# Expert results in a routed feed-forward layer: indirect scatter to (token, choice) rows in place of indirect gathers

## Chip, cores and metric

One core of a Trainium2 chip runs the whole kernel. The metric is the device time of one execution in microseconds (us).

## What is computed

A decoder layer on 2048 tokens (32 sequences of 64) of width 256: self-attention, cross-attention to a compressed context, then a mixture of 8 experts, each added to the residual x. The change touches the last part:

```python
probs = softmax(layernorm(x) @ Wr)                # 8 experts
topk_w, topk_idx = top_k(probs, 2)
topk_w = topk_w / sum(topk_w)
for i in range(8):
    h = silu(xn @ Wg[i]) * (xn @ Wu[i])           # 256 -> 256
    output += w_i * (h @ Wd[i])                   # w_i is 0 where i was not chosen
x = x + output
```

## The kernel before

The five engines' programs are written out by hand (functions tensor, vector, scalar, gpsimd, sync) and meet at semaphores; each runs its own in order. 16 token tiles of 128 tokens pass through attention in blocks of four. Routing of block b (`route_step`) runs beside the cross-attention of the next block: `route_slots` gives each (token, choice) a row in the DRAM table `slots`, where each expert has a region, and POOL scatters the normalised tokens there (`scatter`, two indirect DMAs a token tile, 32 in all). Part 0 is blocks 0 to 2 (12 token tiles), part 1 is block 3. `table(q)` works out on VectorE which expert and which row of `slots` each of the part's expert tiles has (31 tiles in part 0, 15 in part 1), on one partition. `slots` is filled beforehand with arbitrary numbers, so that a tile's unused rows hold something finite.

The expert stage is a loop over 46 expert tiles i of 128 rows. Work on tile i is spread over several iterations:

- PE: `gate_up(i)` (6 matmuls of 512 columns), transposes of h of tile i-1 (`h_T`), `down(i-2)` (6 of 256 columns), transposes of the rows of tile i+2 (`x_T`).
- ACT: `silu(i)`, `h_high(i-1)`, `copy_out(i-2)` into `ys[i % 4]`, `x_high(i+2)`.
- DVE: `gated(i)`, `h_low(i-1)`, `x_low(i+2)`, routing steps of block 3, then from iteration COMBINE_AT = 37 on `combine(i-37)`: two scalar_tensor_tensor instructions add the two weighted result rows of a token tile to x.
- SP: `store(i-2)` of `ys` back to the same rows of `slots`, then `load(i+6)` of the rows of tile i+6 into `xs[(i+6) % 4]` as soon as `x_T(i+2)` has read that buffer (`w.wait_ge(t_xT, i - 3)` inside `load`). Every eighth tile (8, 16, 24, 31, 39) SP first reads a run of row numbers into registers (`load_run`, L342); PE does so for the weights' offsets. `result` stores the finished x.
- POOL: the eight scatters of block 3, one a tile, then `gather(t)`: two indirect DMAs a token tile fetch the rows of its two choices from `slots` into eight buffers `gb`. For t below 12 it waits for the stores of part 0 and is paced by `x_T(36 + t)`; for t of 12 to 15 it waits for the stores of all 46 tiles.

All helpers record one line each: matmuls stand under L354, transposes under L363. L1439 is gated, L1443 h_low, L1433 x_low, L1451 combine, L1713 silu, L1718 h_high, L1723 copy_out, L1708 x_high, L1932 store, L1927 load, L1938 result, L1810 scatter, L1846 gather, L1885 the fill of `slots`.

Of the kernel before, what the change touches and what calls it, by code (L numbers as in the profile page):

```python
# [36 lines left out]
def constants():  # L37
# [36 lines left out]
    c["iota"] = np.tile(np.arange(TILES[0])[None, :], (P, 1))  # L74
    c["power"] = np.tile(np.array([[-0.5] * NT + [0.5] * NT]), (P, 1))
# [70 lines left out]
def decoder(nc, a, const_dram, const_at, out):  # L146
    with ExitStack() as ctx:
# [69 lines left out]
        after_folds = max(w2.at, keep.at + 4 * E * WE + 18 * 4 * D)  # L217
# [8 lines left out]
        past, pastgap = compared("past", [1, TILES[0], E]), compared("pastgap", [1, TILES[0], E])  # L226
# [12 lines left out]
        mxhat = s4("mxhat", [P, 4, D])  # L239
        mxT = s4("mxT", [P, KD, 512])  # L240
        full = s4("full", [1, E, CAP[0] // P])
        ntile = s4("ntile", [1, E])
        upto = s4("upto", [1, E, E])
        ends = s4("ends", [1, E])
        gap = s4("gap", [1, E])
        expert = s4("expert", [1, TILES[0]])
        rowf = s4("rowf", [1, TILES[0]])
        eoff = s4("eoff", [1, sum(TILES)], I32)
        row = s4("row", [1, sum(TILES)], I32)
# [28 lines left out]
        xs = [s6(f"xs{i}", [P, D]) for i in range(4)]  # L278
# [9 lines left out]
        gb = [s7(f"gb{i}", [P, D]) for i in range(8)]  # L288
        assert s7.at <= after_scores
        slots = [nc.dram_tensor(f"slots{i}", (ROWS[i], D), F32, kind="Internal").ap() for i in range(2)]  # L290
# [6 lines left out]
        d_xs, d_ys, d_gb = ([sem(f"d_{n}{i}") for i in range(k)] for n, k in (("xs", 4), ("ys", 4), ("gb", 8)))  # L297
# [33 lines left out]
        t_xT, t_xh, t_xl, t_proj, t_silu, t_gu, t_hT, t_hh, t_hl, t_down, t_y, t_comb = (  # L331
            sem("t_xT"), sem("t_xhigh"), sem("t_xlow"), sem("t_proj"), sem("t_silu"), sem("t_gu"), sem("t_hT"), sem("t_hhigh"),
            sem("t_hlow"), sem("t_down"), sem("t_y"), sem("t_comb"))
# [12 lines left out]
        RK = 24  # L346
# [569 lines left out]
        def vector(e):  # L916
# [271 lines left out]
            def route_norm(b):  # L1188
                w.wait_ge(r_rstd, b + 1)
                w.wait_ge(d_scat, 128 * b)  # L1190
                w.wait_ge(r_xT, b)
                for t in range(4):
                    last = e.tensor_scalar(mxhat[:, t, :], tile(4 * b + t), mmv[:, t, 0:1], mrstd[:, t:t + 1], ALU.subtract, ALU.mult)
                last.then_inc(r_xhat, 1)
# [55 lines left out]
            def route_slots(b):  # L1250
                at = RK * b
                pos = pos_bank(b)[:, 32:64].rearrange("p (t n) -> p t n", n=E)
                base = C("ebase")[:, E * (b == 3):E * (b == 3) + E]
                w.wait_ge(r_pos, b + 1)
                e.tensor_tensor(slot[:, :, :], pos, in_tiles(base, 4), ALU.add).then_inc(r_route, 1)
                w.wait_ge(r_route, at + 18)
                for k in range(2):
                    e.scalar_tensor_tensor(pick[k][:, :, :], rank[:, :, :], float(k), slot[:, :, :], ALU.is_equal, ALU.mult).then_inc(r_route, 1)
                for k in range(2):
                    w.wait_ge(r_route, at + 19 + k)  # L1260
                    e.tensor_reduce(slotf[:, :, k], pick[k][:, :, :], AX, ALU.add).then_inc(r_route, 1)
                w.wait_ge(r_route, at + 22)
                e.tensor_copy(index[:, 4 * b:4 * b + 4, :], slotf[:, :, :]).then_inc(r_route, 1)

            def route_count(b):
                w.wait_ge(r_route, RK * b + 23)
                count = pos_bank(b)[0:1, 64:64 + E].rearrange("p (n o) -> p n o", o=1).broadcast_to([1, E, CAP[0] // P])
                e.tensor_tensor(full[:, :, :], count, in_tiles(C("fill")[0:1], E), ALU.is_gt).then_inc(r_route, 1)
# [6 lines left out]
            def table_ends(q):  # L1275
# [5 lines left out]
                e.tensor_tensor(upto[:, :, :], C("le")[0:1].rearrange("p (i j) -> p i j", j=E), in_tiles(ntile[:, :], E), ALU.mult)  # L1281
# [4 lines left out]
                number = C("iota")[0:1, 0:n].rearrange("p (n o) -> p n o", o=1).broadcast_to([1, n, E])  # L1286
                e.tensor_tensor(past[:, 0:n, :], number, in_tiles(ends[:, :], n), ALU.is_ge).then_inc(r_tab, 1)

            def table_rows(q):
                n, at = TILES[q], 10 * q  # L1290
                mine = slice(FIRST[q], FIRST[q] + n)
                w.wait_ge(r_tab, at + 4)
                e.tensor_reduce(expert[:, 0:n], past[:, 0:n, :], AX, ALU.add)
# [5 lines left out]
                e.scalar_tensor_tensor(row[:, mine], C("iota")[0:1, 0:n], float(P), rowf[:, 0:n], ALU.mult, ALU.add).then_inc(r_tab, 4)  # L1299
# [135 lines left out]

            def gated(i):
# [22 lines left out]
            for i in range(tiles + 2):  # L1459
# [282 lines left out]
        def gpsimd(e):  # L1742
# [62 lines left out]
            def scatter(b, n):  # L1805
                q = int(b == 3)
                t, k = divmod(n, 2)
                w.wait_ge(r_route, RK * b + 23)
# [53 lines left out]
        def sync(e):
# [130 lines left out]
```

## Time and profile before

| | |
|---|---|
| median of 3 runs | 711.88 us (711.37 to 712.47) |
| the profiled execution | 710.46 us |
| its span, first to last instruction | 708.7 us |
| mean granted TensorE clock | 0.962 |
| busy: PE / DVE / ACT / POOL | 638.3 / 494.5 / 348.8 / 242.1 us |
| DMA | 61.54 MB, mean 87 GB/s |

A busy time is a sum over stages with different limits; times of the trace count from the span's start. The expert loop's first tile starts near 554 us, its last result tile is copied out at 690 us.

### The profile page before, as it was taken

What the parts mean: (1) busy time and instruction counts of PE and PEld (TensorE: products, weight loads), DVE (VectorE), ACT (ScalarE), POOL (GpSimd) and SP (SyncE); (2) the same over time, 40 slices, a digit from 0 to 9 for tenths busy, and PEclk for the clock granted to TensorE, in tenths of its full rate; (3) what the DMA queues carried; (4) which work ended last, traced back from release to release, by engine and by line L of the source; (5) the groups of instructions that cost most, each with busy time, mean ns of one, the idle gap of its engine ahead of it and who ended that gap; (6) DMA issues with size and microseconds to landing.
All of it is one profiled execution on the core that took longest, in us unless ns stands there. A gap on an engine that the chain in (4) does not pass through costs nothing.

```text
span 708.7 us, 15301 instructions
## 1 busy us (share of the span) xinstructions
PE 638.3 (90%) x5650; PEld 474.7 (67%) x5650; DVE 494.5 (70%) x1152; ACT 348.8 (49%) x1207; POOL 242.1 (34%) x219
## 2 busy tenths in 40 slices
PE   3787999998899999999999999999979999999850
PEld 2466777777787757667577666775656788888740
DVE  4998989995566878449884698736978737443652
ACT  1477989997660017501374014722288464554420
POOL 2112000000008528534287453773454001302644
PEclk9999999996999999999999999999989999999985
DMA  8699920000000000000001200011171223533544
GB/s 294 161 355 420 417 92 1 3 1 2 1 18 16 1 1 2 2 16 1 2 2 46 75 1 1 2 60 46 39 254 61 67 82 112 156 100 119 160 148 138
DMA packets 49897, 61.54 MB, mean 87 GB/s; under 512 B 15521, under 2 KB 42401, under 8 KB 49569
## 3 DMA queue, kind: packets, MB, share of 16 engines
q1 hardware_dynamic: 45088, 50.88, 21.5%
q0 software_dynamic: 3072, 8.39, 3.9%
q10 hardware_dynamic: 1664, 1.31, 0.7%
q8 instruction: 46, 0.75, 0.5%
q14 instruction: 27, 0.21, 0.1%
HBM read 29.37 MB, written 31.20 MB: 85 GB/s over the span
## 4 chain that ended last, share of the span: by engine, by line
PE 75%; DVE 8%; ACT 8%; issue 4%; DMA 2%; another core or an unknown queue 1%; POOL 1%; ACTq 0%; POOLq 0%; DVEq 0%
PE bank L354 65%; PE bank L363 10%; ACT kbd L1524 2%; ACT vbd L1510 1%; DMA lncol<-in_L_attn_ln_kv_b 1%; DVE wlo L1391 1%; DMA gb<-slots,index 1%; ACT ex L1534 1%; ACT xth L1490 1%; ACT ex L1650 1%; POOL gb L1846 1%; DVE thl L1443 0%; DVE m L1114 0%; DVE gu L1439 0%
## 5 line engine op out<-in xcount | busy, mean ns | idle before, releaser
L1114 DVE TENSOR_TENSOR m<-bank,cst 128x512 f32<-128x512 f32 x192 | 122.0, 684 | 38.4 <-PE bank L354 37.1
L1796 POOL TENSOR_TENSOR r<-m,m 128x512 f32<-128x512 f32 x80 | 104.5, 1330 | 114.9 <-DVE m L1114 95.1
L1650 ACT ACTIVATE ex<-bank,nmax 128x64 f32<-128x64 f32 x256 | 73.2, 337 | 27.0 <-DVE nmax L1357 27.0
L354 PE MATMUL bank<-xth,wbh 128*128 128x512 f32 x192 | 79.9, 416 | 1.1 <-DVE m L1114 1.1
L354 PE MATMUL bank<-xth,wbl 128*128 128x512 f32 x192 | 75.2, 392 | 0.0
L354 PE MATMUL bank<-xtl,wbh 128*128 128x512 f32 x192 | 75.1, 391 | 0.0
L1633 ACT ACTIVATE qc<-bank 128x512 f32<-128x512 f32 x32 | 17.4, 595 | 103.0 <-PE bank L354 103.0
L354 PE MATMUL bank<-wop,qc 128*128 128x256 f32 x256 | 62.5, 389 | 0.3 <-DVE x L1386 0.2
L354 PE MATMUL bank<-r,wqk 64*64 64x512 f32 x512 | 57.7, 594 | 0.0
L354 PEld LDWEIGHTS bank<-wop,qc 128*128 128x128 f32 x256 | 46.4, 189 | 15.6 <-issue 9.2
L1534 ACT ACTIVATE ex<-bank,nmax 128x64 f32<-128x64 f32 x256 | 54.3, 360 | 1.6 <-DVE nmax L1016 1.5
L1810 POOL DMA_INDIRECT slots<-mxhat,index x32 | 32.9, 1029 | 55.6 <-PE bank L363 49.6
L1650 ACT ACTIVATION_READ_ACCUMULATOR ex<-bank,nmax 128x1 f32 x216 | 49.6, 230 | 0.0
L1846 POOL DMA_INDIRECT gb<-slots,index x32 | 30.3, 948 | 55.2 <-PE bank L363 31.9
L354 PEld LDWEIGHTS bank<-xth,wbh 128*128 128x128 f32 x192 | 36.0, 188 | 19.0 <-issue 10.1
L1816 POOL TENSOR_TENSOR ex<-ex,inv 128x512 f32<-128x512 f32 x32 | 33.4, 1045 | 40.7 <-DVE inv L1367 40.3
L363 PE MATMUL bank<-cst,ex 128*128 128x128 f32 x256 | 42.1, 289 | 5.5 <-ACT ex L1534 3.4
L1439 DVE TENSOR_TENSOR gu<-bank,sg 128x256 f32<-128x256 f32 x46 | 19.4, 422 | 37.9 <-ACT sg L1713 30.7
L1761 POOL TENSOR_TENSOR x<-x,borow 128x512 f32<-128x512 f32 x8 | 10.1, 1270 | 104.4 <-DVE xhat L948 78.9
L363 PEld LDWEIGHTS bank<-cst,ex 128*128 128x128 f32 x256 | 30.0, 146 | 18.8 <-issue 8.7
L354 PE MATMUL bank<-whi,txh 128*128 x92 | 40.1, 436 | 2.5 <-issue 1.6
L354 PEld LDWEIGHTS bank<-xth,wbl 128*128 128x128 f32 x192 | 36.0, 188 | 8.2
(217 smaller groups left out, 1484.9 us busy)
## 6 DMA issues: line engine op xcount, KB each, us to landing
slots<-cst SPq DMA_DIRECT2D x1, 13312.0 KB, 44.1
xs<-slots SPq DMA_DIRECT2D x46, 128.0 KB
slots<-ys SPq DMA_DIRECT2D x46, 128.0 KB
slots<-cst SPq DMA_DIRECT2D x1, 5120.0 KB, 49.7
wo_s<-in_L_xattn_Wo SPq DMA_DIRECT2D x1, 2048.0 KB, 18.2
wq_s<-in_L_xattn_Wq SPq DMA_DIRECT2D x1, 2048.0 KB, 11.7
wraw<-in_L_ffn_Wg SPq DMA_DIRECT2D x8, 256.0 KB, 3.8
wraw<-in_L_ffn_Wu SPq DMA_DIRECT2D x8, 256.0 KB, 4.0
```

The lines of the kernel that those rows point to most:

```text
L354: return e.matmul(o, l, r, start=start, stop=stop, skip_group_check=True)
L363: last = e.transpose(o, i, ident)
L1114: last = e.tensor_tensor(m4[n % 2][m][:, :].rearrange("p (b s) -> p b s", s=S), products[half][:, :].rearrange("p (b s) -> p b s", s=S), t ...
L1439: e.tensor_tensor(gu[i % 2][:, :], bank[1 + i % 2][:, F:2 * F], sg[i % 2][:, :], ALU.mult).then_inc(t_gu, 1)
L1524: last = e.activation(kbd[p2][:, :, 2 * t:2 * t + 2, 64 * h2:64 * h2 + 64], bank[0][:, 256:512].rearrange("p (t b l) -> p t b l", t=2, b=2 ...
L1534: last = e.activation(ex[u][:, h * 64:(h + 1) * 64], bank[3 + u % 2][:, h * 64:(h + 1) * 64], ACT.Exp, bias=nmax[u][:, h:h + 1], scale=1.0)
L1633: e.activation(qc[:, 2 * g + pair, :], latent_banks(blk, g)[pair][:, :], ACT.Copy).then_inc(c_qb, 1)
L1650: last = e.activation(ex[b % 4][:, h * 64:(h + 1) * 64], score_banks(b)[odd][:, n * 64:(n + 1) * 64], ACT.Exp, bias=nmax[b % 4][:, 4 * odd ...
L1796: last = e.tensor_tensor(rope[n % 6][half][:, :], m4[n % 2][first][:, :], m4[n % 2][second][:, :], op)
L1810: e.indirect_dma_start(out=slots[q][:, :], out_offset=bass.IndirectOffsetOnAxis(ap=index[:, 4 * b + t, k:k + 1], axis=0), in_=mxhat[:, t, ...
L1816: e.tensor_tensor(segments(ex[b % 4]), segments(ex[b % 4]), per_head(inv[b % 2]), ALU.mult).then_inc(c_exn, 1)
L1846: e.indirect_dma_start(out=gb[n % 8][:, :], out_offset=None, in_=slots[q][:, :], in_offset=bass.IndirectOffsetOnAxis(ap=index[:, t, k:k + ...
```

## The change

- `slots` rows get two more numbers (258 instead of 256 floats): the number of the (token, choice) row, less the choice, and the slot of the token's first choice. `mxhat` and `xs` widen with them, and `route_slots` writes them with two more DVE instructions a block. The fill of `slots` now comes from a constant input array in DRAM of the tables' shape, which gives unused rows a number past the real ones and a slot of -1.
- A new DRAM tensor `results` has a row for each (token, choice), and spare rows for the unused ones. VectorE works out per tile with `places(i)`, one [128 x 1] instruction, where each row of the tile belongs: token row, plus 1 if the slot that holds it isn't the first choice's. For that `table` runs on 128 partitions, with two more instructions (`own`).
- POOL's `store(i)`: one indirect DMA scatters `ys[i % 4]` to those rows of `results`. SP stores tiles no more. POOL's gathers are gone.
- SP's `results_load(t)` reads the two rows of each token of tile t, which now lie side by side, by one plain DMA into one of four buffers `gb` [128, 2, 256].
- `load(i)` also waits for `places(i-4)`, since that reads `xs`.

```diff
+            def places(i):
+                w.wait_ge(t_xT, i + 1)
+                w.wait_ge(r_tab, 10 * (part_of(i) + 1))
+                x = xs[i % 4]
+                e.scalar_tensor_tensor(place[:, i:i + 1], x[:, D + 1:D + 2], own[:, i:i + 1], x[:, D:D + 1], ALU.not_equal, ALU.add).then_inc(t_place, 1)
...
             def combine(t):
                 for k in range(2):
-                    n = 2 * t + k
-                    w.wait_ge(d_gb[n % 8], 16 * (n // 8 + 1))
-                    w.wait_ge(t_comb, n)
-                    e.scalar_tensor_tensor(tile(t), gb[n % 8][:, :], share[:, t, k:k + 1], tile(t), ALU.mult, ALU.add).then_inc(t_comb, 1)
+                    w.wait_ge(d_gb[t % 4], 16 * (t // 4 + 1))
+                    w.wait_ge(t_comb, 2 * t + k)
+                    e.scalar_tensor_tensor(tile(t), gb[t % 4][:, k, :], share[:, t, k:k + 1], tile(t), ALU.mult, ALU.add).then_inc(t_comb, 1)
...
                 if i + 2 < tiles:
                     x_low(i + 2)
+                if i < tiles:
+                    places(i)
                 route_step(3, i, ROUTE_LAST)
...
-            def gather(t):
-                q = int(t >= 12)
-                for k in range(2):
-                    n = 2 * t + k
-                    w.wait_ge(t_comb, n - 7)
-                    e.indirect_dma_start(out=gb[n % 8][:, :], out_offset=None, in_=slots[q][:, :],
-                                         in_offset=bass.IndirectOffsetOnAxis(ap=index[:, t, k:k + 1], axis=0)).then_inc(d_gb[n % 8], 16)
+            def store(i):
+                w.wait_ge(t_place, i + 1)
+                w.wait_ge(t_y, i + 1)
+                e.indirect_dma_start(out=results[:, :], out_offset=bass.IndirectOffsetOnAxis(ap=place[:, i:i + 1], axis=0),
+                                     in_=ys[i % 4][:, :], in_offset=None).then_inc(d_ys[i % 4], 16)
...
+            for i in range(sum(TILES)):
+                n = i - ROUTE_LAST["slots"]
+                if 0 <= n < 8:
+                    w.wait_ge(t_xT, ROUTE_LAST["slots"] + 4 + n)
+                    scatter(3, n)
+                store(i)
...
-            for d in slots:
-                some = cst[:, 0:4 * D].rearrange("p (o d) -> p o d", o=1).broadcast_to([P, d.shape[0] // (4 * P), 4 * D])
-                e.dma_start(d.rearrange("(p n r) d -> p n (r d)", p=P, r=4), some).then_inc(d_fill, 16)
+            for n, d in enumerate(slots):
+                rows = a["fill"][sum(ROWS[:n]):sum(ROWS[:n + 1]), :]
+                e.dma_start(d.rearrange("(p n r) d -> p n (r d)", p=P, r=4), rows.rearrange("(p n r) d -> p n (r d)", p=P, r=4)).then_inc(d_fill, 16)
...
             def load(i):
                 q = part_of(i)
                 w.wait_ge(t_xT, i - 3)
+                w.wait_ge(t_place, i - 3)
...
-            def store(i):
-                q = part_of(i)
-                w.wait_ge(t_y, i + 1)
-                e.dma_start(slots[q][bass.ds(at[i], P), :], ys[i % 4][:, :]).then_inc(d_ys[i % 4], 16)
+            rv = results[0:2 * NT * P, :].rearrange("(t p k) d -> p t k d", p=P, k=2)
+
+            def results_load(t):
+                done = TILES[0] if t < 12 else sum(TILES)
+                for j in range(4):
+                    w.wait_ge(d_ys[j], 16 * len(range(j, done, 4)))
+                w.wait_ge(t_comb, 2 * (t - 3))
+                e.dma_start(gb[t % 4][:, :, :], rv[:, t, :, :]).then_inc(d_gb[t % 4], 16)
...
             for i in range(tiles + 2):
-                if i >= 2:
-                    store(i - 2)
                 if i + 6 < tiles:
                     load(i + 6)
+                if 0 <= i - COMBINE_AT + 2 < 12:
+                    results_load(i - COMBINE_AT + 2)
                 if i in (COMBINE_AT + 5, COMBINE_AT + 9):
                     result(i - COMBINE_AT - 5, i - COMBINE_AT - 1)
-            for lo, hi in ((8, 13), (13, 14), (14, 15), (15, 16)):
-                result(lo, hi)
-            w.wait_ge(d_out, 16 * 6)
+            result(8, 12)
+            for t in range(12, NT):
+                results_load(t)
+            for t in range(12, NT):
+                result(t, t + 1)
+            w.wait_ge(d_out, 16 * 7)
```

How the queue of SP stands in iterations 35 to 40 of the expert loop, before (`slots1<-ys` is store, `xs<-slots1` load; t_y is the count of copied-out tiles):

```order
L1932 DMA slots1<-ys1_211 128x256 [waits t_y]
L1927 ISA [waits t_xT]
L1927 DMA xs1_193<-slots1 128x256
L1932 DMA slots1<-ys2_212 128x256 [waits t_y]
L1927 ISA [waits t_xT]
L1927 DMA xs2_194<-slots1 128x256
L1932 DMA slots1<-ys3_213 128x256 [waits t_y]
```

and in the changed kernel (t_place is the count of `places`, `gb<-results` is results_load):

```order
L1939 ISA [waits t_place,t_xT]
L1939 DMA xs1_195<-slots1 128x258
L1948 DMA gb0_216<-results 128x512 [waits d_ys2,d_ys3,d_ys1,d_ys0]
L1939 ISA [waits t_place,t_xT]
L1939 DMA xs2_196<-slots1 128x258
L1948 DMA gb1_217<-results 128x512
L1939 ISA [waits t_place,t_xT]
L1939 DMA xs3_197<-slots1 128x258
L1948 DMA gb2_218<-results 128x512
```

The stores have left this queue; the loads of results stand behind the loads of rows, and those wait for t_place.

VectorE in the iterations of the first combines, in the changed kernel (the numbers behind names are buffers):

```order
L1455 TENSOR_TENSOR gu_207<-bank,sg_205 128x256 [waits t_hT,t_silu]
L1459 TENSOR_TENSOR thl_210<-bank,thh_208 128x256 [waits t_hhigh]
L1442 TENSOR_TENSOR txl_203<-bank,txh_200 128x256 [waits t_xhigh]
L1450 SCALAR_TENSOR_TENSOR place<-xs_197,own 128x1 [waits t_xT]
L1466 SCALAR_TENSOR_TENSOR x<-gb_218,share,x 128x256 [waits t_comb,d_gb2]
L1466 SCALAR_TENSOR_TENSOR x<-gb_218,share,x 128x256 [waits t_comb]
```

Before, the fourth row wasn't there, and each of the last two waited for a gather of its own (d_gb0 to d_gb7); now `places` of a tile stands just ahead of that iteration's combine.

## Rows read from the trace of the kernel before

**Rows 1.** Page, chain that ended last: by engine, then by line.
```profile
PE 75%; DVE 8%; ACT 8%; issue 4%; DMA 2%; another core or an unknown queue 1%; POOL 1%; ACTq 0%; POOLq 0%; DVEq 0%
```
**Rows 2.** Stretches: us, busy (x count) PE, PEld, DVE, ACT, POOL, PEclk, DMA share, GB/s.
```profile
600.00:640.00 40.00, 38.81 (x243) 33.52 (x242) 18.90 (x53) 19.87 (x62) 6.71 (x7) 1.00 0.43 129
660.00:680.00 20.00, 18.23 (x108) 14.70 (x107) 12.56 (x32) 7.78 (x24) 12.42 (x15) 1.00 0.60 175
```
**Rows 3.** Timeline of ACT: silu (sg), copy_out (ys); start us, us, instruction [idle before].
```profile
636.06 0.38 ACT L1713 ACTIVATE sg<-bank 128x256 f32<-128x256 f32 x1 [0.96 <-PE bank L354]
639.66 0.38 ACT L1713 ACTIVATE sg<-bank 128x256 f32<-128x256 f32 x1 [2.02 <-PE bank L354]
...
652.39 0.38 ACT L1713 ACTIVATE sg<-bank 128x256 f32<-128x256 f32 x1 [0.96 <-PE bank L354]
...
684.57 0.38 ACT L1713 ACTIVATE sg<-bank 128x256 f32<-128x256 f32 x1 [3.23 <-remote]
...
689.65 0.38 ACT L1723 ACTIVATE ys<-bank 128x256 f32<-128x256 f32 x1 [1.00 <-PE bank L354]
```
**Rows 4.** Timeline of POOL: last scatter of block 3, two early gathers.
```profile
616.44 0.96 POOL L1810 DMA_INDIRECT slots<-mxhat,index  x1 [1.58 <-PE bank L363]
...
653.08 0.95 POOL L1846 DMA_INDIRECT gb<-slots,index  x1 [0.30 <-issue]
655.37 0.94 POOL L1846 DMA_INDIRECT gb<-slots,index  x1 [1.35 <-remote]
```
**Rows 5.** Chain that ended last, from the last copied-out tile: start us, us, what.
```profile
690.06 2.39 DMA slots<-ys
...
693.20 0.94 POOL gb L1846
...
701.95 2.80 DMA gb<-slots,index
...
704.77 0.48 DVE x L1451
```
**Rows 6.** Timeline of DVE, gated and x_low of iteration 34, a later pair of combines.
```profile
647.71 0.43 DVE L1439 TENSOR_TENSOR gu<-bank,sg 128x256 f32<-128x256 f32 x1 [0.92 <-ACT sg L1713]
...
648.91 0.43 DVE L1433 TENSOR_TENSOR txl<-bank,txh 128x256 fp32r<-128x256 f32 x1 [0.44 <-ACT txh L1708]
...
668.40 1.06 DVE L1451 SCALAR_TENSOR_TENSOR x<-gb,share,x 128x256 f32<-128x256 f32 x2
```
**Rows 7.** Timeline of SP: stores and loads; the load at 648.28 follows a run.
```profile
643.54 0.35 SPq L1932 DMA_DIRECT2D slots<-ys  x1
644.08 0.33 SPq L1927 DMA_DIRECT2D xs<-slots  x1
646.08 0.36 SPq L1932 DMA_DIRECT2D slots<-ys  x1
648.28 0.33 SPq L1927 DMA_DIRECT2D xs<-slots  x1
```
**Rows 8.** Page, DMA issues: queue, operation, count, KB each, median us to landing.
```profile
slots<-cst SPq DMA_DIRECT2D x1, 13312.0 KB, 44.1
...
wraw<-in_L_ffn_Wg SPq DMA_DIRECT2D x8, 256.0 KB, 3.8
...
ctxs<-in_ctx SPq DMA_DIRECT2D x8, 128.0 KB, 3.0
...
wr<-in_L_ffn_Wr SPq DMA_DIRECT2D x1, 8.0 KB, 1.9
```
**Rows 9.** Stretches of PE: us, PE busy (x count), PEclk, DMA share, GB/s.
```profile
512.00:517.70 5.70, 3.48 (x92) 1.00 0.95 307
517.70:524.50 6.80, 5.81 (x108) 0.50 1.09 358
...
679.60:685.00 5.40, 0.30 (x3) 0.99 0.43 132
```
**Rows 10.** Page, DMA queues: packets, MB, share of 16 engines.
```profile
q8 instruction: 46, 0.75, 0.5%
```

More of the change, by code:

```diff
@@ L225, in decoder @@
         cmpa, cmpb = s4("cmpa", [P, 4, E, E]), s4("cmpb", [P, 4, E, E])
-        past, pastgap = compared("past", [1, TILES[0], E]), compared("pastgap", [1, TILES[0], E])
+        past, pastgap = compared("past", [P, TILES[0], E]), compared("pastgap", [P, TILES[0], E])
         assert compared.at <= s4.at
@@ L238, in decoder @@
         mrstd = s4("mrstd", [P, 4])
-        mxhat = s4("mxhat", [P, 4, D])
+        mxhat = s4("mxhat", [P, 4, D + 2])
         mxT = s4("mxT", [P, KD, 512])
[L241 to L249, printed above, removed]
+        full = s4("full", [P, E, CAP[0] // P])
+        ntile = s4("ntile", [P, E])
+        upto = s4("upto", [P, E, E])
+        ends = s4("ends", [P, E])
+        gap = s4("gap", [P, E])
+        expert = s4("expert", [P, TILES[0]])
+        rowf = s4("rowf", [P, TILES[0]])
+        eoff = s4("eoff", [P, sum(TILES)], I32)
+        row = s4("row", [P, sum(TILES)], I32)
+        own = s4("own", [P, sum(TILES)])
+        place = s4("place", [P, sum(TILES)], U32)
         kept = Space(nc, s4.at)
@@ L277, in decoder @@
         s6 = Space(nc, keep.at + 4 * E * WE)
-        xs = [s6(f"xs{i}", [P, D]) for i in range(4)]
+        xs = [s6(f"xs{i}", [P, D + 2]) for i in range(4)]
         txh = [s6(f"txh{i}", [P, KD, P], F32R) for i in range(3)]
@@ L287, in decoder @@
         ys = [s7(f"ys{i}", [P, D]) for i in range(4)]
-        gb = [s7(f"gb{i}", [P, D]) for i in range(8)]
+        gb = [s7(f"gb{i}", [P, 2, D]) for i in range(4)]
         assert s7.at <= after_scores
-        slots = [nc.dram_tensor(f"slots{i}", (ROWS[i], D), F32, kind="Internal").ap() for i in range(2)]
+        slots = [nc.dram_tensor(f"slots{i}", (ROWS[i], D + 2), F32, kind="Internal").ap() for i in range(2)]
+        results = nc.dram_tensor("results", (2 * NT * P + sum(ROWS) + 1, D), F32, kind="Internal").ap()
         d_cst, d_x0, d_x1, d_w1, d_ln = sem("d_cst"), sem("d_x0"), sem("d_x1"), sem("d_w1"), sem("d_ln")
@@ L296, in decoder @@
         d_fill, d_scat = sem("d_fill"), sem("d_scat")
-        d_xs, d_ys, d_gb = ([sem(f"d_{n}{i}") for i in range(k)] for n, k in (("xs", 4), ("ys", 4), ("gb", 8)))
+        d_xs, d_ys, d_gb = ([sem(f"d_{n}{i}") for i in range(k)] for n, k in (("xs", 4), ("ys", 4), ("gb", 4)))
         s_phase = sem("phase")
@@ L1192, in route_norm @@
                 for t in range(4):
-                    last = e.tensor_scalar(mxhat[:, t, :], tile(4 * b + t), mmv[:, t, 0:1], mrstd[:, t:t + 1], ALU.subtract, ALU.mult)
+                    last = e.tensor_scalar(mxhat[:, t, 0:D], tile(4 * b + t), mmv[:, t, 0:1], mrstd[:, t:t + 1], ALU.subtract, ALU.mult)
                 last.then_inc(r_xhat, 1)
@@ L1262, in route_slots @@
                 w.wait_ge(r_route, at + 22)
+                e.tensor_scalar(mxhat[:, :, D], C("rows2"), 2.0 * 4 * P * b, None, ALU.add).then_inc(r_route, 1)
+                e.tensor_copy(mxhat[:, :, D + 1], slotf[:, :, 0]).then_inc(r_route, 1)
                 e.tensor_copy(index[:, 4 * b:4 * b + 4, :], slotf[:, :, :]).then_inc(r_route, 1)
             def route_count(b):
-                w.wait_ge(r_route, RK * b + 23)
-                count = pos_bank(b)[0:1, 64:64 + E].rearrange("p (n o) -> p n o", o=1).broadcast_to([1, E, CAP[0] // P])
-                e.tensor_tensor(full[:, :, :], count, in_tiles(C("fill")[0:1], E), ALU.is_gt).then_inc(r_route, 1)
+                w.wait_ge(r_route, RK * b + 25)
+                count = pos_bank(b)[:, 64:64 + E].rearrange("p (n o) -> p n o", o=1).broadcast_to([P, E, CAP[0] // P])
+                e.tensor_tensor(full[:, :, :], count, in_tiles(C("fill"), E), ALU.is_gt).then_inc(r_route, 1)
             def table(q):
@@ L1292, in table_rows @@
                 w.wait_ge(r_tab, at + 4)
+                e.tensor_scalar(own[:, mine], C("iota")[:, 0:n], float(P), C("part"), ALU.mult, ALU.add)
                 e.tensor_reduce(expert[:, 0:n], past[:, 0:n, :], AX, ALU.add)
@@ L1298, in table_rows @@
                 w.wait_ge(r_tab, at + 6)
-                e.scalar_tensor_tensor(row[:, mine], C("iota")[0:1, 0:n], float(P), rowf[:, 0:n], ALU.mult, ALU.add).then_inc(r_tab, 4)
+                e.tensor_tensor(own[:, mine], own[:, mine], rowf[:, 0:n], ALU.add).then_inc(r_tab, 1)
+                e.scalar_tensor_tensor(row[:, mine], C("iota")[:, 0:n], float(P), rowf[:, 0:n], ALU.mult, ALU.add).then_inc(r_tab, 3)
                 w.wait_ge(r_tab, at + 10)
@@ L1988 @@
     at["_"] = n
+    fill = np.zeros((sum(ROWS), D + 2), dtype=np.float32)
+    fill[:, D] = 2 * NT * P + np.arange(sum(ROWS))
+    fill[:, D + 1] = -1.0
+    aps["fill"] = give("fill", fill)
     const = give("constants", np.ascontiguousarray(np.concatenate(parts, axis=1)))
```

26 lines of the change are left out of this document (9 added, 17 removed).

## Prediction

> **What bounds the kernel now.** I read the chain that ended last first: PE holds 75% of it [rows 1], so a change to data movement pays only where PE waits. The change works in the expert loop and in the tail, so next come the stretches: from 600 to 640 us PE is busy 38.81 of 40 us at full granted clock, from 660 to 680 only 18.23 of 20, while DMA rises from 129 to 175 GB/s [rows 2]. The silu instructions on ACT mark the pitch of the loop, one a tile. Undisturbed it is 2.55 us (two stores, one a tile, start at 643.54 and 646.08 [rows 7]), PE's own work. Between the silus at 636.06 and 639.66 it is 3.60: tile 31, where PE loads a run of offsets [rows 3]. From 652.39 (tile 36) to 684.57 (tile 45) nine tiles take 32.18 us. Nine undisturbed ones take 22.9, a run's 0.9 more makes 23.8, so **8.4 us are lost** there. What is new in this stretch are gathers, two a tile, issued four in a row about 1.25 us apart; after the fourth, 0.95 us at 653.08, the next one starts at 655.37, 1.35 us idle and released by nothing that the profile can name [rows 4]. Scatters, one a tile, ran up to 616.44 [rows 4], inside the stretch in which PE was 97% busy [rows 2], so one indirect DMA a tile costs nothing.
>
> The tail: the last tile is copied out from 689.65 to 690.03 [rows 3], the span ends at 708.7, so it is **18.7 us**: 2.39 for the store, then eight gathers from 693.20, one every 1.25 us, the last landing 2.80 us after its issue at 701.95, the last combine from 704.77 to 705.25 [rows 5], and 3.45 us until its row block is out.
>
> **The gathers removed.** Taking the 32 gathers away gives back the 8.4 us, if they cause them and the stores don't take their place: **-8.4**. Both bounds are kept: 0 (the stores do the same) and -8.4.
>
> **The stores moved to POOL.** 46 indirect DMAs of about 0.96 us [rows 4], one per 2.55 us; beside the eight scatters two per tile, about 2.5 us, which POOL and the four `ys` buffers can just carry. A buffer is needed again after four tiles, 10.2 us, and a store takes about 3.2 (below). Cost on the path: 0 in the loop.
>
> **The loads of results, now on SP.** This is the largest term. In iterations 35 to 39 SP first does `load(41)` to `load(45)`. `load(41)` waits for `places(37)`, which VectorE runs in iteration 37; only then comes `results_load(0)`; and VectorE's next instruction after `places(37)` is `combine(0)`, which waits for just that load. So in five iterations, 37 to 41, VectorE stands still for a whole trip: SP's release and register move 0.3 (a load follows a store that started 0.54 earlier and issues for 0.35 [rows 7], so 0.2 at least), issue of the row load 0.33, then the results load to landing. For its 256 KB before had only 3.0 us for 128 KB and 3.8 for 256 KB in queued batches, 1.9 for 8 KB and 2.39 for a store of 128 KB [rows 5, 8]. I take 2.4, since the queue is nearly empty and the store is the nearest row; bounds 1.9 and 3.8. With 0.1 for wake-up that is 3.1 us. VectorE's own round is gated, h_low, x_low with 0.35, 0.35 and 0.43, places 0.12 (the narrow end of its instructions, estimated), and two combines 1.06 [rows 6]: 2.3 us. Round: 5.4 us against 2.55. **5 x 2.9 = +14.5** (bounds 5 x 2.3 = +11.5 and 5 x 4.3 = +21.5). PE can run at most one `gate_up` ahead of a standing VectorE, so the wait is not hidden, but the lead (1.0) and the run at tile 39 (0.9) fall inside it: **-1.9**. From t = 5 on no row load is left and the results run ahead.
>
> Here the Trainium skill has a rule (DMA: Bandwidth & Descriptors, section on the anatomy of one DMA): an issued DMA costs about 2.0 us plus bytes over 436 GB/s. For 256 KB that is 2.6 us, and the term would be +15.5 instead of +14.5. For the 128 KB store it gives 2.3, and the trace has 2.39, so the two agree where they can be compared.
>
> **The loads of rows, later than before.** `load(i)` used to follow `x_T(i-4)`, 10 us ahead of its use. Now it follows `places(i-4)`: two pitches (5.1 us) before `x_T(i)`, less 0.9 from x_T to x_low, 0.43 and 0.12. Of the 3.65 left, release, move, issue and landing take 0.5 + 2.2, so about 0.9 is free. With a run of row numbers in front the load at 648.28 came 2.20 us after its store, another 0.54 [rows 7]: 1.66 more, 0.8 over what is free. Five tiles have a run, the first of them where the loop is slow anyway: **+2.0** (bounds 0 and 5).
>
> **VectorE's additions.** Two `own` instructions of some 0.17 us in `table(0)`, where the chain runs over VectorE, and 46 `places` that PE's pitch hides but for the first tiles: **+0.6**. The two writes into `mxhat` a block lie beside PE: 0; should VectorE be late there they cost 0.3 a block. Rows of 1032 bytes instead of 1024: 0, as the DMA share is 0.43 [rows 2].
>
> **The tail.** Release 0.5 (a gather came 0.75 after its store landed), the indirect store 3.2 (0.96, then 2.2 for the write to land, next to 2.39 for the plain store [rows 5]): 3.7. The first results load lands 2.6 later; four loads are issued within 1.6, so VectorE's 4 x 1.07 sets the end: 6.9. Then 3.45 as now. 14.05 against 18.7: **-4.6** (bounds -3 and -6).
>
> **The clock.** The granted clock fell to 0.50 (1.2 GHz) at 517.7 after a stretch in which PE was busy 3.48 of 5.70 us, and just after the idle stretch of 679.6 to 685.0 [rows 9]. In the five waiting rounds PE is busy 2.55 of 5.4, so a fall is likely there. At 1.2 GHz PE needs 5.1 per tile, which the rounds cover; the last three tiles after them it would cost 3.9 us. Half of that: **+2** (bounds -2.1, as the present last tile already ran at 1.2 GHz, and +4).
>
> **The fill**, 13.3 and 5.1 MB, lands 44 us after its issue [rows 8] and is needed only by the first scatters, in the second block of cross-attention: 0, even if copying from DRAM to DRAM takes twice as long.
>
> Sum: -8.4 + 14.5 - 1.9 + 2.0 + 0.6 - 4.6 + 2 = **+4.2**. Against the profiled execution's 710.46 this gives 714.7; the median of the three runs is 1.4 above that execution, so I forecast **716.1 us**, of its own range 711 to 723.
>
> **Rivals.**
>
> *The trips are short* (0.20, faster). Landing 1.9, row loads never late, the clock stays up: -8.4 + 11.5 - 1.9 + 0.3 - 4.6 - 2.1 = -5.2, 706.7 us. For it: SP is idle and the DMA queues are half empty. Against it: each bound has to come out at its good end. With the other terms as forecast the sign turns at a round of 4.6 us.
>
> *VectorE doesn't stand at all* (0.05, faster). If something lets the results run ahead, -8.4 - 4.6 - 2.1 + 2.6 remain: 699.4 us. The order of the two queues speaks against it.
>
> *Indirect stores disturb as gathers do* (0.10, slower). The loss was 8.4 us over some 20 gathers issued in the loop, 0.4 each; with about half of that for the less dense stores, on some 40 tiles outside the waiting rounds, +8 and nothing given back beyond what the rounds cover: 724 us. Against it stand the scatters, one a tile without loss [rows 2, 4].
>
> *The fill holds up code loading* (0.06, slower). 46 instruction packets of 16 KB came in over the span [rows 10], one per 15 us, so three to six fall into the fill, whose pieces are now 53.7 KB by the access pattern, where the old ones were 4 KB. At a sixteenth of the 358 GB/s of a full DMA stretch [rows 9] such a piece takes 2.4 us, so up to +6 to +12 before 130 us; I price it at +6 on top of the forecast, 722 us. The Trainium skill says in the same page's section on queues that an engine changes queues only at packet boundaries, which is this mechanism; no row here shows it, as instruction packets took a share of 0.5% before.
>
> *The terms cancel* (0.07): within 0.2% of 711.88, about what a measurement of this kernel can tell from no change.
>
> **How the numbers follow.** The forecast has 0.52, with its tail just under 0.2% at 0.02. Slower: 0.50 + 0.10 + 0.06 = 0.66; same 0.07 + 0.02 = 0.09; faster 0.25. The range 702 to 726 takes in all but the case of no standing and the extreme ends of the bounds.
>
> **What would show it.** In the changed kernel's timeline: x<-gb on DVE idle about 3 us before each of the first five combines, ended by the DMA gb<-results, and silus about 5.4 us apart there; silus at 2.55 before it except at runs, where they lengthen by up to 0.8 over now; POOL's results<-ys at 0.96 us each; a tail of about 14 us. If the five waits are absent or under 2 us, the main term is wrong; if pitches of 3.5 us alternate with 2.57 all along, the stores disturb like gathers; if PE's waits on "issue" grow before 130 us, the fill does it.

## The result, and the profile after

The changed kernel takes **720.61 us** (median of 4 runs, 719.24 to 723.09) where the kernel before takes 711.68 beside it (711.37 to 712.47): a ratio of **1.0128, 95% interval 1.0098 to 1.0157**. That is +8.9 us, slower as forecast, but about twice the +4.2 that the prediction gave. The profiled execution took 719.24 with a span of 717.4, and is compared below with the 708.7 of before.

The silu copies on ACT, in the timeline of the changed kernel, for tiles 16, 17, 22, 24, 36 and 45:

```profile
598.28 0.39 ACT L1730 ACTIVATE sg<-bank 128x256 f32<-128x256 f32 x1 [0.96 <-issue]
602.89 0.39 ACT L1730 ACTIVATE sg<-bank 128x256 f32<-128x256 f32 x1 [2.60 <-remote]
...
620.62 0.38 ACT L1730 ACTIVATE sg<-bank 128x256 f32<-128x256 f32 x1 [3.99 <-remote]
...
626.51 0.39 ACT L1730 ACTIVATE sg<-bank 128x256 f32<-128x256 f32 x1 [2.35 <-issue]
...
658.79 0.38 ACT L1730 ACTIVATE sg<-bank 128x256 f32<-128x256 f32 x1 [0.97 <-issue]
...
700.11 0.39 ACT L1730 ACTIVATE sg<-bank 128x256 f32<-128x256 f32 x1 [1.01 <-PE bank L359]
```

In the kernel before tile 16 stands at 599.77 and tile 24 at 620.78; tiles 36 and 45 are in [rows 3]. So the span divides like this:

| stretch | before | after | difference |
|---|---|---|---|
| start to tile 16 | 599.77 | 598.28 | -1.5 |
| tile 16 to 24 | 21.01 | 28.23 | **+7.2** |
| tile 24 to 36 | 31.61 | 32.28 | +0.7 |
| tile 36 to 45 | 32.18 | 41.32 | **+9.1** |
| tile 45 to its copy out | 5.08 | 3.76 | -1.3 |
| copy out to the end | 19.05 | 13.53 | -5.5 |
| span | 708.7 | 717.4 | +8.7 |

**Tile 36 to 45** is where the forecast put its largest term. The chain of waits of the changed kernel there (start, us, what) shows one standing round after another:

```profile
669.00 0.41 DVE thl L1459
669.42 0.33 DVE txl L1442
...
670.09 0.34 SPq L1939
...
670.48 2.76 DMA gb<-results
673.26 0.50 DVE x L1466
...
675.60 0.33 SPq L1939
...
675.98 2.85 DMA gb<-results
...
687.05 3.85 DMA gb<-results
690.93 0.49 DVE x L1466
```

The row load (L1939) goes out 0.21 us after the place is written, the results load 0.39 behind it, and VectorE's combine starts when it lands. The rounds from combine to combine are 5.51, 5.59, 5.47 and 6.61 us against the forecast of 5.4. In VectorE's timeline the waits are 3.79, 3.38, 3.46, 3.34 and 4.48 us. The view of groups of instructions, from 554 to 705 us, has them in one row, and the places beside them:

```profile
L1466 DVE SCALAR_TENSOR_TENSOR x<-gb,share,x 128x256 f32<-128x256 f32 x23 | 11.1, 483 | 19.1 <-DMA gb<-results 18.5
L1450 DVE SCALAR_TENSOR_TENSOR place<-xs,own 128x1 uint32<-128x1 f32 x46 | 9.7, 211 | 0.0
```

**Tile 16 to 24** was forecast at no change. POOL's timeline there:

```profile
605.05 0.96 POOL L1861 DMA_INDIRECT results<-ys,place  x1 [2.36 <-ACT ys L1740]
606.32 0.96 POOL L1827 DMA_INDIRECT slots<-mxhat,index  x1 [0.30 <-ACT ys L1740]
607.58 0.96 POOL L1861 DMA_INDIRECT results<-ys,place  x1 [0.30 <-issue]
608.85 0.96 POOL L1827 DMA_INDIRECT slots<-mxhat,index  x1 [0.31 <-issue]
611.97 0.96 POOL L1861 DMA_INDIRECT results<-ys,place  x1 [2.16 <-ACT ys L1740]
```

A store and a scatter take 2.53 us, the pitch is 2.55, so they join into unbroken rows (of 4, 4, 6 and 3 here), as the gathers did in [rows 4]. PE is busy 22.68 of 28.00 us from 598 to 626, where the kernel before kept it busy 22.62 of 23.00 from 598 to 621. With one store a tile and nothing else, the pitch stays at 2.55 (648.59 to 658.79 for tiles 32 to 36).

The longest hold is before the silu of tile 22, which starts at 620.62. The last of the six matmuls that it waits for is this one, from PE's timeline:

```profile
616.04 0.40 PE L359 MATMUL bank<-whi,txl 128*128 x1
```

It is done at 616.44, so ACT starts 4.18 us late; PE meanwhile runs out of inputs and stands from 619.05 to 621.93. Behind that the granted clock is lower (same columns as [rows 2]):

```profile
621.90:626.00 4.10, 3.99 (x15) 3.24 (x16) 1.82 (x6) 1.36 (x4) 2.88 (x3) 0.59 0.40 102
```

3.99 us of work at 0.59 would be 2.35 at full speed. So 1.6 of the 7.2 us, an estimate, are a slower PE behind the wait and not the wait itself.

**The tail**, in the chain of waits of the changed kernel from 701 us:

```profile
701.03 0.39 ACT ys L1740
...
702.17 0.84 POOL results L1861
...
703.72 0.59 POOL results L1861
...
705.01 2.69 DMA results<-ys,place
...
707.76 3.07 DMA gb<-results
710.86 0.50 DVE x L1466
```

The last tile is copied out from 703.87 to 704.25 and its store is the third of three queued on POOL. The tail from 704.25 is 13.15 us, against 18.7 before and 14.05 forecast.

### The profile page after: what moved, and what is told of

It reads as the page before. It is cut to its first block, busy times and chain, and to the rows that moved or that the text cites. A ratio compares the mean times of both kernels' runs of the same rounds, so it can differ in the third digit from the quotient of the medians.

```text
span 717.4 us, 15360 instructions
## 1 busy us (share of the span) xinstructions
PE 644.7 (90%) x5650; PEld 478.7 (67%) x5650; DVE 501.6 (70%) x1210; ACT 350.9 (49%) x1207; POOL 256.4 (36%) x233
## 4 chain that ended last, share of the span: by engine, by line
PE 71%; DVE 8%; ACT 8%; DMA 6%; issue 3%; SPq 2%; another core or an unknown queue 1%; POOL 0%; POOLq 0%; ACTq 0%; DVEq 0%
PE bank L359 61%; PE bank L368 10%; DMA gb<-results 3%; DMA wkv_s<-in_L_xattn_w_kc_kv 2%; ACT kbd L1541 2%; ACT vbd L1527 1%; ACT ex L1667 1%; DVE wlo L1400 1%; DVE x L1466 1%; SPq L1881 1%; ACT ex L1551 1%; DMA xs<-slots 1%; ACT xth L1507 1%; DVE thl L1459 0%
## 5 line engine op out<-in xcount | busy, mean ns | idle before, releaser
L1861 POOL DMA_INDIRECT results<-ys,place x46 | 44.5, 968 | 92.8 <-ACT ys L1740 90.4
L359 PE MATMUL bank<-whi,txh 128*128 x92 | 42.1, 458 | 2.3 <-issue 1.3
L1730 ACT ACTIVATE sg<-bank 128x256 f32<-128x256 f32 x46 | 17.8, 386 | 52.1 <-PE bank L359 28.7
## 6 DMA issues: line engine op xcount, KB each, us to landing
slots<-in_fill SPq DMA_DIRECT2D x1, 13416.0 KB, 53.7
slots<-in_fill SPq DMA_DIRECT2D x1, 5160.0 KB, 61.8
```

The lines of the kernel that those rows point to most:

```text
L359: return e.matmul(o, l, r, start=start, stop=stop, skip_group_check=True)
L1730: e.activation(sg[i % 2][:, :], bank[1 + i % 2][:, 0:F], ACT.Silu).then_inc(t_silu, 1)
L1861: e.indirect_dma_start(out=results[:, :], out_offset=bass.IndirectOffsetOnAxis(ap=place[:, i:i + 1], axis=0), in_=ys[i % 4][:, :], in_offs ...
```

## Experiments

The open questions were whether the five waits are worth what they seem, what costs 7.2 us from tile 16 to 24, and what the gathers had cost. All time ratios are to the kernel before on the same chip.

**1. Results loads first.** In SP's loop:

```
-                if i + 6 < tiles:
-                    load(i + 6)
-                if 0 <= i - COMBINE_AT + 2 < 12:
-                    results_load(i - COMBINE_AT + 2)
+                if 0 <= i - COMBINE_AT + 4 < 12:
+                    results_load(i - COMBINE_AT + 4)
+                if i + 6 < tiles:
+                    load(i + 6)
```

> The changed kernel with results_load(t) two iterations earlier and ahead of that iteration's row load on SP; nothing else. Theory (VectorE stands in five combines for a load that SP issues only after a place): the five waits of 3.34 to 4.48 us are gone, the nine tiles from tile 36 to 45 take about 24 us instead of 41.3, the granted clock stays up, and the time falls by 15 to 18 us to 703 to 706. Rival (the loads of 256 KB are late because the queues are full, or indirect stores disturb PE all along): waits stay or the pitch stays above 3 us, time 714 or more.

Measured 704.40 (702.78 to 707.88), ratio 0.9911 [0.988, 0.9942]. No combine in the loop waits any more, and tiles 36 to 45 take 24.92 us instead of 41.32. The order on SP's queue was worth 16.4 us in these nine tiles (15.4 by the ratios of the whole kernel) of a change whose whole effect was +8.9. Tiles 16 to 24 still take 27.53.

**2. Scatters on two tiles in three.**

```
-                n = i - ROUTE_LAST["slots"]
-                if 0 <= n < 8:
-                    w.wait_ge(t_xT, ROUTE_LAST["slots"] + 4 + n)
+                n = {14: 0, 15: 1, 17: 2, 18: 3, 20: 4, 21: 5, 23: 6, 24: 7}.get(i)
+                if n is not None:
+                    w.wait_ge(t_xT, i + 4)
                     scatter(3, n)
```

> The changed kernel with the eight scatters of block 3 on two tiles in three (three tiles hold five indirect DMAs instead of six), so that POOL is not filled by them. Theory (a long unbroken row of indirect DMAs on POOL holds up PE's completion signals): the 7.2 us lost from tile 16 to 24 shrink to 0 to 3, time 714 to 717. Rival (what counts is the number of indirect DMAs, not their crowding): 720 to 721. Rival (the loss comes from something else in these iterations, such as places or the load of run numbers): no change either.

Measured 717.81, ratio 1.0118 [1.0089, 1.0146]. The spread scatters reach to tile 27; from tile 16 to 27 it takes 31.68 us, against 35.87 in the changed kernel and 28.65 before. 4.2 of 7.2 come back with the same number of DMAs, so 3.0 stay, at the edge of what was expected. The whole time came out above the expected 714 to 717, and the ratio's interval overlaps that of the changed kernel: the gain shows in the tiles of the profiled execution, not in the total.

**3. The kernel before, each scatter of block 3 twice.**

```
+                if b == 3:
+                    e.indirect_dma_start(out=spare[:, :], out_offset=bass.IndirectOffsetOnAxis(ap=index[:, 4 * b + t, k:k + 1], axis=0),
+                                         in_=mxhat[:, t, :], in_offset=None).then_inc(d_spare, 16)
```

> The kernel before with each of block 3's eight scatters issued twice, the second into a DRAM tensor that nothing reads; stores stay on SP. It does extra work that the computation doesn't need. Theory (two indirect DMAs per tile back to back disturb PE's signals): plus 5 to 8 us, 717 to 720, lost between tiles 17 and 25, with waits of ACT or DVE of 2 to 4 us whose releaser the profile can't name. Rival (the loss in the changed kernel comes from ys buffers or from the store's latency): 711.7 to 712.5.

Measured 714.73, ratio 1.0067 [1.0045, 1.0089]. The sixteen come in four unbroken rows of four; tiles 16 to 35 take 52.69 us instead of 50.07. So the loss appears in the kernel before too, but at 2.6 us it is half the least I expected.

**4. The kernel before with plain loads for gathers.**

```
-                    e.indirect_dma_start(out=gb[n % 8][:, :], out_offset=None, in_=slots[q][:, :],
-                                         in_offset=bass.IndirectOffsetOnAxis(ap=index[:, t, k:k + 1], axis=0)).then_inc(d_gb[n % 8], 16)
+                    e.dma_start(gb[n % 8][:, :], slots[q][P * (n % 8):P * (n % 8 + 1), :]).then_inc(d_gb[n % 8], 16)
```

> The kernel before with the 32 gathers replaced by plain loads of 128 KB from fixed rows on the same queue, at the same places; the result rows read are not those of the tokens. Theory (gathers cause the 8.4 us lost from tile 36 to 45): these nine tiles take about 24 us instead of 32.18, and the tail shortens by 1 to 3 because a plain issue is shorter: 700 to 703.5. Rival (VectorE's combines or the DMA traffic itself cause it): nine tiles still take over 30 us, 709 to 712.

Measured 696.61, ratio 0.9805 [0.978, 0.983]: more than expected. Tiles 36 and 45, to be read against [rows 3]:

```profile
653.55 0.38 ACT L1713 ACTIVATE sg<-bank 128x256 f32<-128x256 f32 x1 [0.96 <-PE bank L354]
...
677.04 0.38 ACT L1713 ACTIVATE sg<-bank 128x256 f32<-128x256 f32 x1 [1.00 <-PE bank L354]
```

Nine tiles in 23.49 us instead of 32.18: **-8.7**, where the prediction's first term was -8.4. The rest of the gain is 1.3 in the last tile and 4.7 in the tail, more than I had expected of it: the last eight loads are issued in 4.30 us, where eight gathers took 9.70. The plain loads also go out in pairs, mostly with over 1 us between them, so the experiment removes the indirect DMAs and their unbroken rows at once.

**5. Places two iterations earlier** (in the changed kernel, SP's order untouched):

```
                 if i + 2 < tiles:
                     x_low(i + 2)
-                if i < tiles:
-                    places(i)
+                    places(i + 2)
```

with `places(0)` and `places(1)` behind the first two `x_low`.

> The changed kernel with places(i+2) right behind x_low(i+2) in place of places(i), so a place is written two iterations earlier and load(i+6) no longer waits for VectorE's running iteration; SP's order is as changed. Theory: load(41) to load(45) pass at once, the results loads behind them leave two tiles before their combines, the five waits go as in the run with the results loads first, and the tiles with a run of numbers give back the 0.7 us each that they took more than before: 701 to 704.5. Rival (the results loads must be ahead of the row loads to be in time): waits of 1 to 3 us remain, 707 to 715.

Measured 702.59, ratio 0.9882 [0.9837, 0.9927]. Silus of tiles 16, 24, 36 and 45:

```profile
600.47 0.39 ACT L1731 ACTIVATE sg<-bank 128x256 f32<-128x256 f32 x1 [0.97 <-issue]
...
628.18 0.39 ACT L1731 ACTIVATE sg<-bank 128x256 f32<-128x256 f32 x1 [2.03 <-issue]
...
659.86 0.39 ACT L1731 ACTIVATE sg<-bank 128x256 f32<-128x256 f32 x1 [0.97 <-issue]
...
683.45 0.39 ACT L1731 ACTIVATE sg<-bank 128x256 f32<-128x256 f32 x1 [1.00 <-PE bank L359]
```

Nine tiles in 23.59: the waits go without touching SP's order, so it was the row load's wait for the place that held the results load, as the prediction had it. Around the runs of numbers for tiles 31 and 39, tiles 30 and 38 take 2.56 us instead of 3.20 and 3.22 in experiment 1, and tiles 31 and 39 take 0.2 and 0.6 less: 2.1 us for the later row loads of two runs.

**6. The kernel before, its eight scatters in one unbroken row**, by one number: all wait for `x_T` of tile 20.

```
-                w.wait_ge(t_xT, ROUTE_LAST["slots"] + 4 + n)
+                w.wait_ge(t_xT, ROUTE_LAST["slots"] + 7)
```

> The kernel before with the same eight scatters, held until x_T of tile 20 and then issued in one unbroken row (1.26 us each, 10 us) instead of one a tile. No DMA more, none fewer. Theory (crowding of indirect DMAs on POOL holds up completion signals): 2 to 6 us lost between tiles 19 and 25, 713 to 717. Rival (their number counts, or their traffic): no loss, 710.5 to 712.

Measured 715.45, ratio 1.0055 [1.0027, 1.0084]. Same DMAs, same number; tiles 16 to 35 take 55.14 us instead of 50.07, **+5.1**. The timeline of all engines shows what is held:

```profile
606.91 1.04 POOL L1810 DMA_INDIRECT slots<-mxhat,index  x1 [46.25 <-PE bank L363]
...
608.05 0.38 ACT L1713 ACTIVATE sg<-bank 128x256 f32<-128x256 f32 x1 [0.96 <-PE bank L354]
...
608.98 0.38 ACT L1723 ACTIVATE ys<-bank 128x256 f32<-128x256 f32 x1 [0.27 <-PE bank L354]
...
610.17 0.39 PE L354 MATMUL bank<-whi,txl 128*128 x1
...
611.21 0.28 PE L354 MATMUL bank<-whi,thl 128*128 x1
...
612.58 0.38 ACT L1713 ACTIVATE sg<-bank 128x256 f32<-128x256 f32 x1 [2.94 <-remote]
...
615.84 0.96 POOL L1810 DMA_INDIRECT slots<-mxhat,index  x1 [0.30 <-issue]
616.14 0.38 ACT L1723 ACTIVATE ys<-bank 128x256 f32<-128x256 f32 x1 [2.91 <-PE bank L354]
```

At 608.98 ACT starts 0.04 after PE's last matmul of the tile (608.66 + 0.28). At 612.58 the silu starts 2.02 us after the last matmul that it waits for (610.17 + 0.39). At 616.14 ACT copies out a tile whose last matmul was done at 611.49 (611.21 + 0.28): 4.65 us late, of which ACT stood idle for the last 2.91. PE had finished; its neighbour learned of it late. The eight scatters are those of the kernel before and no store is on POOL, so neither the `ys` buffers nor the number of DMAs can be the cause here. As in the changed kernel, a lower clock follows (0.59 from 618 to 622 us), and its cost is part of the 5.1. In the first 2.8 us of the row no signal is late.

**7. Experiments 1, 2 and 5 together.**

> The changed kernel with three edits together: results loads first and two iterations earlier, places two iterations earlier, scatters on two tiles in three. Theory: 704.4 less 3 to 4 for the scatters less 1 to 2 for the runs = 698.5 to 701.5, faster than the kernel before by 1.3 to 1.8%. Rival (the gains overlap, since row loads and results loads meet): 703 to 705.

Measured 701.62 (699.04 to 703.69), just above the expected 701.5, ratio **0.9848 [0.9805, 0.9892]**. It has the lowest ratio of the versions that compute the whole layer; its interval overlaps that of experiment 5. Tiles 16 to 27 take 31.47, tiles 36 to 45 23.67, so the two gains stand side by side.

**8 and 9. The kernel before, its eight scatters in rows of two and of four**: the wait is for `ROUTE_LAST["slots"] + 4 + 2 * (n // 2)`, and for `... + 4 + 4 * (n // 4)`.

> The kernel before with the eight scatters in pairs, two every second tile; same number. Theory (completion signals are held up only some 3 us into an unbroken row, as the row of eight left the first silu on time): rows of two last 2.2 us, 0 to 0.5 us lost from tile 16 to 27, 710.5 to 712. Rival (two in a row already hold them up): 2 us or more lost.

> The kernel before with the eight scatters in two rows of four, four tiles apart; same number. Theory: rows of four last 4.8 us, so each costs about 1 to 2 us: 2 to 4 lost from tile 16 to 27, 713 to 715. Rival (the loss needs a row longer than five): 0 to 0.5 lost.

Measured 711.07, ratio 0.9975 [0.9955, 0.9995], and 713.14, ratio 1.0006 [0.9988, 1.0025]. By the silus from tile 16 to 35, where the kernel before takes 50.07 us:

| eight scatters in rows of | 1 | 2 | 4 | 8 |
|---|---|---|---|---|
| tiles 16 to 35, us | 50.07 | 49.58 | 51.08 | 55.14 |
| tiles 16 to 23, us | 17.83 | 17.82 | 19.33 | 23.39 |

In the three versions with moved scatters the pitch into tile 24, where a run of numbers is read, is 2.69 instead of 3.18 us; why was not looked for. Up to tile 23, without that, two in a row are free, two rows of four cost 1.5 (1.0 by the longer stretch; less than the 2 to 4 expected, and not to be seen in the ratio), and one row of eight 5.6 (5.1).

**10. Block 3's scatters as plain stores** (on the kernel of experiment 5):

```
+                if q:
+                    e.dma_start(slots[q][P * n:P * (n + 1), 0:D], mxhat[:, t, 0:D]).then_inc(d_scat, 16)
+                    return
```

> The changed kernel with places two iterations earlier, and with block 3's eight scatters replaced by plain stores of 128 KB on POOL's queue to fixed rows of the slots; the last four row blocks of the output are summed from earlier result rows. So block 3's rows don't reach its experts. Theory (the 7.2 us lost from tile 16 to 24 come from scatters and result stores joined into unbroken rows of indirect DMAs): tiles 16 to 27 take 28.6 to 29.5 us as in the kernel before, against 35.3 with places early alone, and the time is 695 to 697.5. Rival (they come from any transfers on POOL's queue there, from places, or from the wider rows): 33 us or more, 701 to 703.

Measured 695.39, ratio 0.9905 [0.988, 0.9931], but the kernel before took 701.36 beside it (701.26 to 704.05), not 711. Tiles 16 to 27 take 28.04 us. That fits the theory and doesn't prove it, for the reason that the next pair shows. (Block 3's rows don't reach its experts here, so it is no version to use.)

**11 and 12. The kernel before and the changed kernel again.**

> The kernel before, profiled again, because its runs beside the last experiment took 701.3 to 704.1 us where they took 708 to 716 beside all others. Theory (that chip gave back the clock earlier, or its gathers didn't hold anything up): if this run is near 701 us, its tiles 36 to 45 or its clock before 200 us show which; if it is near 711 us, the nine tiles take 32.2 us as before and the difference stays open.

> The changed kernel, profiled again beside it. Theory: its five waits and the loss of 7.2 us from tile 16 to 24 are the same whatever the chip: 1.1 to 1.5% over the kernel before where that takes 711 us; some 2% over it where that takes 701 us, if what it gains there are gathers that cost less.

They met a chip of the same kind: the kernel before took 703.47 as a kernel and 701.54 beside it (ratio of one program to itself 1.0017 [1.0000, 1.0034]), the changed kernel 714.33, ratio **1.0171 [1.013, 1.0212]**. Tiles 36 and 45 of the kernel before, and two of its gathers:

```profile
652.68 0.38 ACT L1713 ACTIVATE sg<-bank 128x256 f32<-128x256 f32 x1 [0.96 <-PE bank L354]
...
676.50 0.38 ACT L1713 ACTIVATE sg<-bank 128x256 f32<-128x256 f32 x1 [1.00 <-PE bank L354]
```

```profile
657.13 0.94 POOL L1846 DMA_INDIRECT gb<-slots,index  x1 [0.31 <-issue]
658.38 0.95 POOL L1846 DMA_INDIRECT gb<-slots,index  x1 [0.30 <-DVE x L1451]
```

Its gathers run in an unbroken row of ten (649.56 to 661.8), and the nine tiles take **23.82 us**. Here nothing is held up. The changed kernel's tiles 16, 24, 36 and 45:

```profile
598.98 0.38 ACT L1730 ACTIVATE sg<-bank 128x256 f32<-128x256 f32 x1 [0.97 <-PE bank L359]
...
620.72 0.38 ACT L1730 ACTIVATE sg<-bank 128x256 f32<-128x256 f32 x1 [1.21 <-PE bank L359]
...
653.23 0.38 ACT L1730 ACTIVATE sg<-bank 128x256 f32<-128x256 f32 x1 [0.97 <-PE bank L359]
...
693.89 0.38 ACT L1730 ACTIVATE sg<-bank 128x256 f32<-128x256 f32 x1 [1.01 <-PE bank L359]
```

From tile 16 to 24 it takes 21.74 instead of 28.23, although POOL's rows of indirect DMAs are longer (ten and seven). That is against what was expected, the same 7.2 us lost on any chip. The nine tiles take 40.66, close to the 41.32 of the first chip: the five waits don't depend on it. On such a chip the change costs 10.7 us by the spans (700.4 to 711.1): +16.8 in the nine tiles, where there were no held gathers to win back, +0.7 and +0.9 in the two stretches ahead of them, -1.1 at the start, -6.7 from the last copy out.

Experiment 10 therefore ran where there was nothing to hold up, and its control is void. What stands on experiments 2, 3, 6 and 9 is that crowding costs; that it is the whole of the 7.2 us is an inference from experiment 12, where the same program, with its places and wider rows, loses 0.7 there. On a chip that suffers from it only 4.2 were taken away (experiment 2).

## Why the prediction was right in sign and wrong in size

| step | forecast | shown |
|---|---|---|
| gathers removed | -8.4 | -8.7 (experiment 4) |
| stores on POOL, in the loop | 0 | **+7.2** |
| VectorE's five waits, less their cover | +14.5 - 1.9 = +12.6 | **+17.7** |
| row loads later | +2.0 | +0.7 outside the nine tiles |
| tail | -4.6 | -5.5 |
| clock | +2 | -1.3 in the last tile |
| VectorE's additions | +0.6 | +0.1 from tile 0 to 16 |
| start of the loop | 0 | -1.6 |

The sum was +4.2 and the spans differ by +8.7. Two steps were 12.3 us too low: the stores on POOL, put at nothing, and the five waits, too small. Six others came out 7.9 better than forecast together and hid most of it (the rows of the table add up to 8.6, from rounding). So even the distance of 4.5 us owes something to luck.

**The gathers.** Right, and for the reason given: the nine tiles take 23.5 without them, 23.8 was forecast.

**The stores beside the scatters: this step failed.** The prediction said of two indirect DMAs a tile that POOL and the four `ys` buffers "can just carry" them, and set 0. The room was counted in POOL's busy time alone. [Rows 4] already showed what an unbroken row of 0.30 us gaps does, and the same stretch of the sum blamed four gathers in a row for 8.4 us; two DMAs of 1.26 us in a pitch of 2.55 are such a row. The rival on indirect stores named the mechanism, put it at 0.10, and spread it over forty tiles, where single stores cost nothing; it struck only the eight tiles with two. What the runs show in place of the 0 is 7.2 us from tile 16 to 24, with signals up to 4.18 us late; and on another chip only 0.7, which nothing in the prediction allows for.

**The five waits.** The mechanism, its place and the number of rounds were right, and experiments 1 and 5 each take it away alone. Its size was short by 5.1. Against the nine tiles of experiment 5, the time up to the first combine is 4.0 longer (8.96 against 4.92), the four rounds are 12.4 longer (23.18 against 10.79), and from the fifth combine to tile 45 it is 1.3 longer. Three of the five rounds exceed the pitch by about 3.0, near the forecast 2.9. The first wait costs its full 3.8, since VectorE comes to it with no backlog to work off. The last round is 6.61, because four results loads go out in a row there and the first lands after 3.85. Of the cover of 1.9 only 0.6 is there: the four rounds exceed the pitch of 2.55 by 13.0, and 12.4 are left against experiment 5, whose nine tiles have the run at tile 39 in them. PE's lead covered nothing. So of the missing 5.1, 2.5 are longer rounds, 1.3 the cover and 1.3 the time after the last wait. The landing itself was 2.7 to 3.0, where 2.4 was taken. By the Trainium skill (DMA: Bandwidth & Descriptors, anatomy of one DMA) 256 KB take 2.6 us, an estimate; the page gives that rule for DMAs that GpSimd issues, and these are SyncE's. The trace has 2.72 to 3.02 for the four that were issued singly, so the page was nearer than the row of a 128 KB store that I preferred.

**Row loads.** 0.7 shows outside the waits; experiments 1 and 5 differ by 2.1 over the runs from tile 30 on, so 2.0 was a fair size, but most of it fell where VectorE stood anyway.

**The tail.** The steps hold: from the copy out to the store's landing 3.45 us (forecast 3.7), to the first combine 3.16 more (2.6, as the results load took 3.07), eight combines 4.33 (4.3). The store stood behind two others on POOL, which was missed, yet was issued only 0.76 after the copy out, where 0.5 was taken. What made the tail shorter is its end, 2.21 after the last combine instead of 3.45.

**The clock.** It did fall in the waiting rounds. The view by stretches of the changed kernel from 690 us on (busy us of PE, PEld, DVE, ACT and POOL, then the granted clock, DMA share and GB/s):

```profile
690.00:695.00 5.00, 2.26 (x11) 2.29 (x12) 3.64 (x10) 0.67 (x2) 0.00 (x0) 0.59 0.94 295
695.00:700.00 5.00, 5.00 (x22) 4.00 (x22) 3.19 (x9) 1.56 (x5) 1.11 (x2) 0.73 0.43 130
700.00:705.00 5.00, 3.08 (x23) 2.50 (x21) 4.16 (x11) 2.19 (x6) 2.77 (x3) 1.00 0.67 210
```

By the last tile it was back at full speed (2.4 GHz), while before it ran that tile at half: 3.76 us against 5.08. Experiment 12 has 0.7 less in the nine tiles, at a mean grant of 0.92 from 690 to 699 us. So the term is a small gain, near the good end of its bounds. The same last tile takes 3.76 in experiment 4 too, which has no waiting rounds: half speed there belonged to the tile that stood behind the gathers. And the clock fell where no term had it, behind the wait at tile 22.

**The fill** lands after 53.7 and 61.8 us instead of 44.1 and 49.7, with no effect that shows: PE is as busy in the first 130 us as before (105.8 us against 104.8), so the rival of held-up code loading finds nothing. The -1.5 before tile 16 isn't its work either: from 180 to 185 us the granted clock was 0.82 before and 1.00 after, and tile 0 starts at 561.28 in experiment 7, whose granted clock was 0.93 over the first 100 us against 0.97 before. Repeats of the same code differ by such amounts ahead of the loop.

## What to carry to other kernels

On an in-order queue, a load that someone stands still for must be issued ahead of any load that waits for that someone's later work: moving one line, or the instruction it waits for, was worth 16 us of 720. When work moves to a queue that is free by its busy time, count how the instructions join up, not only whether they fit; single indirect DMAs and pairs of them cost nothing here, rows of four and more did on three chips, and hardly anything on a fourth. Whoever blames a row of such instructions for a loss before must price the rows that the change makes by the same rate.

## What the runs showed of the hardware

- While GpSimd issues indirect DMAs with 0.30 us between them, PE's completion signals reached ACT up to 4.65 us late (experiment 6; 4.18 in the changed kernel). With eight scatters, rows of 1, 2, 4 and 8 cost 0, 0, 1.5 and 5.6 us up to tile 23. Rows of scatters alone do it (experiment 6), and stores mixed with scatters (the changed kernel); of gathers, experiment 4 shows that their 8.7 us go when plain loads take their place. Why it happens, the traces don't tell.
- It isn't so on every chip. In experiments 1 to 9 (three chips) the kernel before took 711 to 712 us, in 10 to 12 (two other chips) 701.4 to 703.5, and the difference sits in the nine tiles with gathers (32.18 against 23.82 us) and in the last tile that follows them. Whether it is the chip itself or how the program and its memory lay on it stays open; so does what versions 5 and 7 would take there.
- An indirect DMA of 128 KB takes 0.96 us of POOL, and 2.7 to 2.9 from issue to landing (2.69 for the last store, 2.80 and 2.94 for gathers before). One column of places on VectorE (128x1) takes 0.21 us, but the next instruction starts 0.12 to 0.14 after it, so on the chain it costs about the 0.12 that was estimated.
